# An attention and expert kernel: the next batch's x loaded and split in another order, and the row maxima placed one per slot

## The reference, cut to what matters

```python
def _L0_attn_ref(x, wq, bq, wk, bk, wv, bv, wo, bo):
    q = proj(wq, bq); k = proj(wk, bk); v = proj(wv, bv)
    scores = jnp.einsum('bhqd,bhkd->bhqk', q, k) / scale
    probs = jax.nn.softmax(scores, axis=-1)
    ctx = jnp.einsum('bhqk,bhkd->bhqd', probs, v)
    return ctx.transpose(0, 2, 1, 3).reshape(B, S, HIDDEN) @ wo.T + bo
```

## Time and profile before

| | |
|---|---|
| median of three runs | 2168.53 us |
| the profiled execution | 2167.16 us |
| its span, first to last instruction | 2165.4 us |
| PE busy | 2053.6 us (95%) |
| DVE, ACT, POOL busy | 1265.8, 866.7, 869.7 us |
| granted TensorE clock, mean share of full | 0.981 |
| attention | roughly the first 1350 us of the span |

### The profile page before, as it was taken

The page is one execution under the profiler, slowest core; times in us unless marked ns, Lnnn a source line. Parts: engine busy times, 40 slices in busy tenths (PEclk is TensorE's granted clock), DMA queues, the critical chain, the costliest instruction groups (busy, mean ns, idle before and its releaser), DMA issues. The chain is left out here.

```text
span 2165.4 us, 29932 instructions
## 1 busy us (share of the span) xinstructions
PE 2053.6 (95%) x9636; PEld 1215.9 (56%) x9637; DVE 1265.8 (58%) x2247; ACT 866.7 (40%) x1530; POOL 869.7 (40%) x828
## 2 busy tenths in 40 slices
PE   7999899999899999899999987789999999999997
PEld 5655455555455555555555433468644444446886
DVE  5777676578676477677477753466222222224875
ACT  2265564366564266565266662321111111112332
POOL 2255564455554455655354554400011111113651
PEclk9999999999999999999999999899999999999999
DMA  5322333313333313333312302671222222224752
GB/s 165 69 50 64 84 75 88 113 37 77 84 74 83 118 31 77 91 75 80 122 28 58 79 12 93 214 282 52 85 88 87 89 94 89 87 82 148 228 179 73
DMA packets 94815, 205.90 MB, mean 95 GB/s; under 512 B 24608, under 2 KB 25120, under 8 KB 92256
## 3 DMA queue, kind: packets, MB, share of 16 engines
q1 hardware_dynamic: 83888, 168.90, 26.8%
q0 software_dynamic: 10800, 35.40, 5.9%
HBM read 113.53 MB, written 39.85 MB: 71 GB/s over the span
## 5 line engine op out<-in xcount | busy, mean ns | idle before, releaser
L852 DVE TENSOR_REDUCE max_half<-ps_side 128x1 f32<-128x512 f32 x1024 | 656.7, 682 | 235.4 <-PE ps_side L600 232.5
L768 ACT ACTIVATE probs_outer<-ps_s 128x512 f32<-128x512 f32 x629 | 365.3, 600 | 204.5 <-PE ps_s L622 173.6
L622 PE MATMUL ps_s<-kq_stack 97*128 97x512 f32 x937 | 399.2, 429 | 28.6 <-ACT probs_outer L768 21.4
L600 PE MATMUL ps_side<-kq_stack 96*128 96x512 f32 x1024 | 404.8, 404 | 2.9 <-DVE max_half L852 2.3
L622 PEld LDWEIGHTS ps_s<-kq_stack 97*128 97x128 f32 x937 | 179.4, 192 | 197.6 <-issue 98.3
L1516 PE MATMUL ps_gu<-gu_sb,xT_e 128*128 x568 | 257.7, 596 | 0.7 <-issue 0.5
L1414 POOL DMA_INDIRECT x_g<-x,who_all x71 | 67.4, 949 | 454.4 <-PE ps_t L1506 358.5
L600 PEld LDWEIGHTS ps_side<-kq_stack 96*128 96x128 f32 x1024 | 196.7, 192 | 53.0 <-DVE max_half L852 18.6
L768 ACT ACTIVATE probs_mid<-ps_s 128x512 f32<-128x512 f32 x308 | 178.4, 600 | 117.2 <-PE ps_s L622 102.2
L536 POOL TENSOR_TENSOR acc<-probs_outer,probs_mid 128x512 f32<-128x512 f32 x129 | 163.7, 1295 | 151.8 <-ACT probs_mid L768 151.8
L536 POOL TENSOR_TENSOR acc<-probs_outer 128x512 f32<-128x512 f32 x129 | 163.1, 1290 | 130.7 <-ACT probs_outer L768 130.7
(11 more groups left out here) (210 smaller groups left out, 3065.9 us busy)
## 6 DMA issues: line engine op xcount, KB each, us to landing
kq_stack<-kq SPq DMA_DIRECT2D x192, 256.0 KB, 5.1
y_slots<-y_t SPq DMA_DIRECT2D x71, 256.0 KB, 2.3
res<-inv_rows SPq DMA_DIRECT2D x128, 64.0 KB, 2.0
probs_outer<-x SPq DMA_DIRECT2D x16, 512.0 KB, 5.1
x_r<-x SPq DMA_DIRECT2D x32, 256.0 KB, 3.8
x_t<-x SPq DMA_DIRECT2D x32, 256.0 KB
gu_sb<-wgu SPq DMA_DIRECT2D x8, 1024.0 KB, 15.7
out<-gu_sb SPq DMA_DIRECT2D x32, 256.0 KB, 2.7
```

Of the source, the lines that this page charges most:

```text
L600: nc.tensor.matmul(bank, q_stack[par][0:3 * HD, h, t * P:(t + 1) * P], k_stack[par][0:3 * HD, h, half * HALF:(half + 1) * HALF], start=Tru ...
L622: nc.tensor.matmul(out, k_stack[par][0:3 * HD + 1, h, kt * P:(kt + 1) * P], q_stack[par][0:3 * HD + 1, h, half * HALF:(half + 1) * HALF], ...
L768: nc.scalar.activation(probs(loc, h), score_bank(b, loc * HG + h)[0], ACT.Exp, scale=HD ** -0.5).then_inc(probs_ready, 1)
L852: nc.vector.reduce_max(max_half[:, u // 2, u % 2:u % 2 + 1], bank, AX.X).then_inc(side_free, 1)
```

## The change

Two things are changed, and nothing is computed otherwise.

**x chunks.** Before, SP loads chunks 0 and 1 at the start of its body of group 1, chunks 2 and 3 there between the second `invert` and `row`, and chunks 4 to 7 at the very end of that body, behind `spread` and the second `row`; ACT takes them one by one after steps 8, 9, 10 and 11 of group 1 and 1, 2, 4 and 5 of group 2. Now chunks 2 and 3 are loaded in group 1's `spread`, behind the transfers of heads 0 and 1; 4 and 5 at the start of group 2's body; 6 and 7 behind its first `invert`. ACT takes chunks 0 and 1 after step 8 of group 1, and the others after steps 0, 1, 4, 5, 7 and 8 of group 2.

**Maxima and their second row.** Slots 12 and 44 lose their second `pre`, slots 61 and 62 get one each, and PE does the second `row` (slot 63) behind the strips of that slot, not ahead of them.

```diff
--- before.py
+++ after.py
@@ -38,14 +38,14 @@
          (49, 49, 50, 50, 51, 51, 52, 52, 53, 53, 54, 55))
 assert all(unit[-1] % (FOLD * SLOTS) == FOLD * SLOTS - 1 for unit in UNITS)
 ROW_SLOTS = (40, 63)
-PRE_TWICE = (12, 28, 44)
-PRE_UNTIL = 61
+PRE_TWICE = (28,)
+PRE_UNTIL = 63
 INVERT = (36, 24)
 PROBS = 3
 FOLD_DVE = 1
 NORM_AFTER, SPLIT_W_AFTER = (15, 9), 13
-X_HIGH = {(1, 8): 0, (1, 9): 1, (1, 10): 2, (1, 11): 3, (2, 1): 4, (2, 2): 5, (2, 4): 6, (2, 5): 7}
-X_AFTER = {(1, 9): (0,), (1, 11): (1, 2, 3), (2, 1): (4,), (2, 3): (5,), (2, 5): (6, 7)}
+X_HIGH = {(1, 8): (0, 1), (2, 0): (2,), (2, 1): (3,), (2, 4): (4,), (2, 5): (5,), (2, 7): (6,), (2, 8): (7,)}
+X_AFTER = {(1, 9): (0, 1), (2, 1): (2, 3), (2, 5): (4, 5), (2, 7): (6,), (2, 9): (7,)}
 
 
 EXPS_BETWEEN = {3: ((0, 0), (0, 1)), 4: ((0, 2),), 5: ((0, 3), (1, 0), (1, 1)), 6: ((1, 2),), 7: ((1, 3),)}
@@ -309,7 +309,7 @@
 
                 for sel in range(2):
                     if g == 0:
-                        sp.wait_ge(x_split, (b + 1) * CHUNKS + 3 + sel)
+                        sp.wait_ge(x_split, (b + 1) * CHUNKS + 1 + sel)
                     elif g == 1:
                         sp.wait_ge(x_split, (b + 1) * CHUNKS + CHUNKS - 1 + sel)
                     else:
@@ -321,8 +321,8 @@
                     c, half = i % C, i // C
                     if i < 2:
                         sp.wait_ge(w_split, 2 * (n - 1) + i + 1)
-                    elif i in (4, 5):
-                        sp.wait_ge(w_split, 2 * n + i - 3)
+                    elif i < 4:
+                        sp.wait_ge(w_split, 2 * n + i - 1)
                     else:
                         sp.wait_ge(x_split, b * CHUNKS + i - 1)
                     sp.sem_inc(passed_sp, 1)
@@ -330,7 +330,7 @@
                                  xT[bass.ds(b, 1), :, c, half * HALF:(half + 1) * HALF].rearrange(
                                      "a p t -> (a p) t")).then_inc(x_in[i % 2], 16)
 
-            def spread(n, par, m=None):
+            def spread(n, par, m=None, between={}):
 
                 sp.wait_ge(proj_free, PROJ * (n + 1))
                 sp.sem_inc(passed_sp, 1)
@@ -341,6 +341,8 @@
                     for r, parts in enumerate((slice(K_HI, Q_HI + 1), slice(K_LO, Q_HI + 1, 2), slice(K_HI, Q_LO + 1, 2))):
                         sp.dma_start(kq_stack[par][r * HD:(r + 1) * HD, :, h, :].bitcast(F32),
                                      kq[h * HD:(h + 1) * HD, parts, :].bitcast(F32)).then_inc(stacked[h], 16)
+                    if h in between:
+                        between[h]()
 
             def send_rows(par, half):
                 to = q_stack[par][3 * HD:3 * HD + 1, :, half * HALF:(half + 1) * HALF]
@@ -370,17 +372,19 @@
                                  inv_rows[h].partition_broadcast(HD)).then_inc(rinv_in, 16)
 
             def body(b, m, g, last):
-                x_chunks = g == 1 and not last
-                if x_chunks:
-                    load_x(b + 1, m + 3, range(2))
+                x_first_half, x_second_half = g == 1 and not last, g == 2 and not last
+                if x_first_half:
+                    load_x(b + 1, m + 3, (0, 1))
+                if x_second_half:
+                    load_x(b + 1, m + 2, (4, 5))
                 if g:
                     invert((b * G + g) * NHALF - 1)
+                if x_second_half:
+                    load_x(b + 1, m + 2, (6, 7))
                 if g == 0:
                     sp.wait_ge(x2_out[7], 16 * (b + 1))
                     sp.sem_inc(passed_sp, 1)
                 invert((b * G + g) * NHALF, g == 0)
-                if x_chunks:
-                    load_x(b + 1, m + 3, range(2, 4))
                 if not (last and g == G - 1):
                     row(m, g, 0, last)
                 if not (last and g > 0):
@@ -391,11 +395,10 @@
                     sp.sem_inc(passed_sp, 1)
                     sp.dma_start(wv_lo[:].bitcast(F32), wv_lo_kept).then_inc(wv_moved, 16)
                 if not (last and g >= G - 2):
-                    spread(m + 2, g % 2, m)
+                    spread(m + 2, g % 2, m, {h: lambda i=h + 2: load_x(b + 1, m + 3, (i,))
+                                             for h in (0, 1)} if x_first_half else {})
                 if not (last and g == G - 1):
                     row(m, g, 1, last)
-                if x_chunks:
-                    load_x(b + 1, m + 3, range(4, CHUNKS))
                 if last and g == 1:
                     sp.wait_ge(w_split, 2 * B * G)
                     sp.dma_start(stage[:], woT[:, 0:2, :]).then_inc(wo_in, 16)
@@ -672,12 +675,17 @@
                             scores(b, loc + 1, slot)
                         if loc == 0 and slot < SIDE_RING:
                             pe.wait_ge(tail_free, b * TAIL + KT - (SIDE_RING - 1 - slot))
-                        for kind, u, place in side_in(last, loc, slot):
-                            side_unit(b, b * G + g, g, kind, u, place)
+                        units = side_in(last, loc, slot)
+                        for kind, u, place in units:
+                            if kind != "row" or u == 0:
+                                side_unit(b, b * G + g, g, kind, u, place)
                         if slot == SLOTS - 1 and loc % FOLD == FOLD - 1:
                             for done in range(loc - FOLD + 1, loc + 1):
                                 weighted(b, done)
                             row_sums(b, loc)
+                        for kind, u, place in units:
+                            if kind == "row" and u == 1:
+                                side_unit(b, b * G + g, g, kind, u, place)
 
             for i in range(2):
                 pe.wait_ge(w_split, 2)
@@ -795,8 +803,8 @@
                             exps(b, loc + 1, slot)
                         for kind, u, place in side_in(last, loc, slot):
                             side_unit(b * G + g, g, kind, u, place)
-                    if (g, loc % STEPS) in X_HIGH and not last:
-                        x_part(b + 1, X_HIGH[g, loc % STEPS])
+                    for i in X_HIGH.get((g, loc % STEPS), ()) if not last else ():
+                        x_part(b + 1, i)
                     if loc % KT == KT - 1:
                         take(b, loc)
```

## The result

The changed kernel takes 2131.86 us (median of 4 runs, 2128.77 to 2136.28), the kernel before 2165.83 us (4 runs, 2160.91 to 2170.02): a ratio of 0.9852, 95% interval 0.9825 to 0.9879. That is faster by 1.5%, well beyond the 0.5% bound. The profiled execution took 2128.77 us, 38.4 less than that of before, where 31.2 were forecast (2167.2 to 2136).

The account below looks back on a forecast made before the run. PE was taken as the bound, busy for 95% of the 2165.4 us span. The terms summed to 2167.2 - 25.2 - 6.6 - 0.3 - 0.3 + 0.8 = 2135.6, said as 2136 us; range 2130 to 2142, with (a) to 2148.

Parts of the forecast that it names:

- the prologue: Before the first scores, last maxima come at DVE's pace; two more there cost +0.8 us.
- The chunks: Groups 1 and 2 of batches 0 to 2: of 32.4 us for x, 7.2 stay, a gain of 25.2 us.
- under 5: Chunk 2, behind three transfers of `spread`, lands in under 5 us from its issue.
- no wait: ACT wants chunk 2 6.1 us after its issue, so it does not wait; 0.3 us remains as cost.
- The end of a group: At slots 60 to 63, strips begin earlier and the next group's score comes 0.15 us earlier.
- Slots 12 and 44: Each loses one `pre` of 0.235 us on PE, together -0.47 us in a group.
- Half of it: Batch 3, group 2, without projections: half of the 0.6 us gain per group, -0.3 us.
- Rival (b): Ends of some 14 groups: DVE's addition loses to POOL's next instruction, 1.3 us later, +18 us, 2154 us; chance 0.07.
- (a): The new places of the chunks are late too: 4 us in each batch, 12 in all, 2148 us; chance 0.12.
- (c): One chunk in each group 2 still stops PE, some 7 us with slow clock, +21, 2157 us; chance 0.05.
- (d): Slower: chunk 6, ahead of the context on ACT, delays all exponentials 1 us for 1 us in three batches; chance 0.02.
- (e): No change: PE's stops are covered by something else that waits just as long; chance 0.03.

Follow-up runs that it names:

- x behind spread: The changed kernel with chunks 2 and 3 of x issued behind all twelve transfers of `spread`; 2170.44 us (one run).
- Slots only: The kernel before with only the places of the maxima changed, the second row still ahead of the strips; 2203.26 us (one run).
- row only: The kernel before with only the second row moved behind the strips, the maxima in their old slots; 2165.57 us (one run).
- fold at slot 0: The changed kernel with DVE's addition of each second step one slot earlier in its program; 2122.84 us (one run).
- norm late: The changed kernel with POOL's `normalise` of the first half moved to step 1 of the next group, save in group 3; 2128.18 us (one run).

## Why the prediction was right

The median, 2131.86 us, lies 4.1 us under the forecast and within the range. In part that is luck: the profile gained 38.4 us where the sum says 31.6. Of the 6.8 us between them 2.9 lie behind the change and 3.1 in the prologue, whose step was wrong; a late end of 1.2 us, which the forecast left out, goes the other way.

**The chunks: right, part by part.** 25.2 us forecast, 25.5 measured. Chunk 2 was to land within 5 us and took 5.4 (219.55 to 224.95; 5.8 and 5.7 in batches 1 and 2), chunk 3 5.5 to 6.5. The view of the six chunks 2 to 7 in batch 0, from issue to landing:

```profile
DMA to landing us min/median/max: 2.9/3.1/5.5
```

ACT took chunk 2 at 226.35, so 1.4 us were left, and it came to chunk 3 as that landed (batch 0) or 0.2 and 0.5 us too early (batches 1 and 2), inside the slack that the prediction gave it: the first two steps of group 2 took 8.43 to 8.44 us in all three batches. So the "under 5" was too low and the "no wait" held for PE; x behind spread shows what lies beyond. The Trainium skill's rule (DMA: Bandwidth & Descriptors, Queues, rings and completion order) that descriptors are consumed in ring order on each DMA engine fits the two chunks that follow three transfers of `spread` each, 5.4 and 5.5 us, beside the 2.9 to 3.1 of the other four. It does not give the length: with all twelve ahead (x behind spread) chunk 2 took 4.5 us. Against the same steps without chunks, chunk 2 cost 0.30 us (0.3 forecast), chunk 4 0.29 (0.3), chunk 6 0.52 (0.5 to 0.6), chunk 7 0.30 (0.4), the pair in group 1 0.82 (0.8).

**The end of a group: right, a little small.** The strips begin 2.08 us behind slot 60's score (before 2.44), the sums at 3.88 (4.18), the next score at 4.91 (5.15): -0.24 us where -0.15 was forecast. The addition asks at 2.39 in place of 2.01 and ends at 3.73 (before 3.72): the same end, as argued, as long as it gets in.

**Slots 12 and 44: the right price where there are projections, the wrong one where there are none.** Step by step, steps 3 and 11 lose 0.21 us each in a normal group (0.235 forecast). In group 2 of batch 3 they lose 0.67 and 0.59, step 15 gets 0.20 longer, and the group gets 1.16 us shorter for a forecast of 0.3. PE there, from the score of slot 12 to that of slot 13, before, the two `pre` in one row:

```profile
1213.94 0.39 PE L622 MATMUL ps_s<-kq_stack 97*128 97x512 f32 x1
1214.17 1.01 PE L600 MATMUL ps_side<-kq_stack 96*128 96x512 f32 x2
1215.02 0.40 PE L622 MATMUL ps_s<-kq_stack 97*128 97x512 f32 x1
```

and after, with one:

```profile
1179.61 0.39 PE L625 MATMUL ps_s<-kq_stack 97*128 97x512 f32 x1
1179.83 0.41 PE L603 MATMUL ps_side<-kq_stack 96*128 96x512 f32 x1
1180.08 0.40 PE L625 MATMUL ps_s<-kq_stack 97*128 97x512 f32 x1
```

Between the two scores 1.08 us pass before and 0.47 after: without projections PE meets DVE's pace of 0.62 us a maximum on a ring of three banks, and a second `pre` costs that, not PE's 0.235. "Half of it" was no working at all: the term should have come from the earlier trace rows.

**The prologue: wrong step.** "Two more cost 2 x (0.62 - 0.235) = +0.8 us" supposed that the last maxima are the bottleneck from the last projection on, and that this projection stays where it was. From the first `pre` to the first score it took 50.9 us in the three kernels with the old slots and 49.85 to 49.92 in the ten profiles with the new: -1.05, not +0.8. Slots only (49.92) and row only (50.91) put this on the slots. DVE took the last projection's low part at 79.10 us after, 82.38 before; counted from the first `pre` (35.27 and 36.30) that is 2.25 us earlier. From there to the transpose of max_q it takes 5.90 us in place of 4.70. So the maxima behind the projection do cost some 1.2 us, as the step said (0.8), but the projection did not stay where it was. That fewer maxima ahead of it are the reason was not tested. Of the other 1.2 us of the 2.3, 1.0 is the start of the first `pre`, which lay between 34.7 and 36.6 us over the profiles.

**Rival (b): not the main case, but real.** It had a chance of 0.07 as an event of 14 groups for 18 us. In fact it happens to some ends and not to others: 1 or 2 of 10 in the changed kernel, 1.2 us each. The step that failed is "it asks before POOL's last addition ends, and got in between then": asking before is not enough. In the changed kernel POOL's running addition still had 0.8 us to go when DVE asked (153.46 against 150.49 + 3.77), before 1.15 us, with fold at slot 0 some 0.2 us, but there with another addition behind it and not `normalise`. At the ends of groups all but one of the losses came at 0.8 us, but the ends of groups 3 never lost at the same 0.8 us, and in norm late an addition lost inside a group that had asked under 0.1 us ahead; so the distance alone is not the rule, and what is stays open. Asking 0.4 or 0.6 us earlier ended them in all but 1 of 50. The other rivals fell: chunk 3 was late for ACT by up to 0.5 us, as (a) has it, but cost PE nothing; no stop is left (c), chunk 6 was 1.54 us late for ACT and cost PE 0.52 (d), and the stops were not covered (e).

## What to carry to other kernels

- A transfer in an in-order queue is as late as what stands ahead of it, not as its own length: look at what the queue's engine issues before it, and slip the urgent one in behind the first few. Then put the instruction that consumes it where other work (here the strips) covers it.
- Two edits can have opposite signs apart (+34 and -5 us) and -12.5 together: when one shortens the path and the other moves a wait off it, test the pair.
- When two engines' instructions contend, their order can change from run to run. Asking clearly earlier, or leaving nothing queued behind on the other engine, stopped the losses at those places here. Compare kernels by groups without a late end before giving up an edit.

## What the hardware showed that I had not expected

DVE's addition (two SBUF inputs) and POOL's don't share their time, they take turns by whole instructions. Wherever the rows above show both, the addition ends 0.54 to 0.56 us after the end of the last POOL instruction that it let pass: before, 157.02 against POOL's third addition at 156.46; in norm late 155.07 against 154.52; where it lost, 156.04 against `normalise` at 155.49. POOL's next instruction, if DVE goes first, is 0.45 us longer (1.74, with fold at slot 0 the third of its additions, the three then 4.21 for 3.77 us); if POOL goes first it keeps its 1.26. So the length that the profile gives the addition, 0.71 to 2.60 us, holds the wait: with POOL idle (at 129.66 us of the changed kernel) it is 0.68 us. The Trainium skill says of the pair, in "Trainium Architecture — The Big Picture", What this means for kernel authors, that it is an exclusive lock and not a split of bandwidth; the trace agrees. Which engine gets the next turn differed between two executions of the same program at the same place (group 1 of batch 0), and no run here settles what decides it.

A stop of PE costs more than itself. In x behind spread, after the 9.36 us (the 3.6 us that follow, then two stretches of 4 us; columns as before):

```profile
236.40:240.00 3.60, 3.49 (x10) 0.50 0.28 73
240.00:244.00 4.00, 4.00 (x25) 0.66 0.23 67
244.00:248.00 4.00, 4.00 (x18) 1.00 0.01 1
```

In the first stretch the granted clock is 0.50, the lower level of 1.2 GHz, and matmuls start 0.43 us apart in place of 0.235; in the third it is back at 1.00. Of the 80.28 us of this group, 66.80 are what it takes in the changed kernel, 9.36 the stop and 1.2 the late end. The 2.9 us left are an estimate of what running slowly cost.
